# Last columns of the scans kept in SBUF: copied to the states by ScalarE instead of VectorE

## What is computed

```
x = x + ga * attn(layernorm(x) * (1 + ca) + sa)       # attn: Mamba forwards and backwards, then a projection
x = x + gb * ffn(layernorm(x) * (1 + cb) + sb)        # ffn: 6-bit block quantization, then x @ w.T + bias

# one Mamba direction, D_INNER = 1024 channels, N = 16 states for each channel
u     = silu(conv4(h @ win_u.T) + bconv)
dbc   = u @ wx.T                                      # gives dt, B and C
delta = softplus(dt @ wdt.T + bdt)
dA    = exp(delta * A)                                # for each channel and state n
dBu   = delta * u * B                                 # for each channel and state n
h_t   = dA_t * h_(t-1) + dBu_t                        # the scan over the rows t
y     = sum over n of h * C
out   = ((y + u * Dp) * silu(z)) @ wout.T
```

## Time and profile before

| | |
|---|---|
| median of 3 runs | 7603.56 us (7603.14 to 7606.13) |
| the profiled execution | 7600.66 us, its span 7598.7 us |
| busy share: PE / DVE / ACT / POOL | 90% / 92% / 80% / 92% |
| scans, L1153 | 4096; DVE waited 363.1 us for exponentials before them |
| copies from SBUF, L1183 | 1024 |
| dBu, L692 | 2048, 4787.8 us busy on POOL |

### The profile page before, as it was taken

One profiled execution on the slowest core, in us unless ns is written; L12 is line 12 of the kernel. 1 busy time (PEld: TensorE's weight loads), 2 busy tenths in 40 slices (PEclk: granted clock), 3 DMA queues, 4 the chain that ended last, 5 costly groups with the idle time before them and its releaser, 6 DMA issues. The chain is left out here.

```text
span 7598.7 us, 137446 instructions
## 1 busy us (share of the span) xinstructions
PE 6830.6 (90%) x32682; PEld 4035.6 (53%) x32682; DVE 6955.4 (92%) x10093; ACT 6069.6 (80%) x11545; POOL 6968.9 (92%) x3774
## 2 busy tenths in 40 slices
PE   6899999899898989999898999999898999999889
PEld 3455555555555555555555555555555555555455
DVE  2799999999999999999999999999999999999766
ACT  1788888888788888888788888888788888888645
POOL 0899999999999999999999999999999999999678
PEclk8999999999999999999999999999999999999999
DMA  8444445444444454444445544444355444444555
GB/s 258 145 137 134 128 139 149 128 120 144 132 134 126 141 150 124 123 143 138 122 129 145 149 113 136 139 137 134 117 150 149 107 141 135 138 130 131 152 193 172
DMA packets 605609, 1066.02 MB, mean 140 GB/s; under 512 B 113584, under 2 KB 221872, under 8 KB 596336
## 3 DMA queue, kind: packets, MB, share of 16 engines
q1 hardware_dynamic: 602704, 1055.84, 46.9%
q10 hardware_dynamic: 2080, 1.05, 0.0%
HBM read 926.61 MB, written 130.05 MB: 139 GB/s over the span
## 5 line engine op out<-in xcount | busy, mean ns | idle before, releaser
L692 POOL TENSOR_TENSOR dBu<-Bb,du 128x1024 f32<-128x1024 f32 x2048 | 4787.8, 2365 | 74.9 <-DVE hV L1153 44.2
L1153 DVE TENSOR_TENSOR_SCAN scans<-scans,state,dBu 128x512 f32<-128x512 f32 x2304 | 2902.8, 1280 | 393.6 <-ACT scans L806 363.1
L806 ACT ACTIVATE scans<-delta,A 128x512 f32<-128x512 f32 x4096 | 2745.7, 691 | 557.4 <-DVE hC L1169 480.9
L1016 PE MATMUL yT<-ident,hC 128*128 128x128 f32 x9216 | 1407.4, 282 | 344.1 <-DVE hC L1169 340.8
L1169 DVE TENSOR_TENSOR hC<-scans,Cb 128x512 f32<-128x512 f32 x2304 | 1556.8, 680 | 12.2 <-PE yT L1016 12.2
L1016 PEld LDWEIGHTS yT<-ident,hC 128*128 128x128 f32 x9216 | 1058.6, 143 | 774.8 <-DVE hC L1169 536.4
L701 POOL TENSOR_TENSOR hR<-hR,Cb 128x512 f32<-128x512 f32 x1024 | 1290.0, 1270 | 190.2 <-DVE state L1183 183.7
L1153 DVE TENSOR_TENSOR_SCAN hR<-scans,state,dBu 128x512 f32<-128x512 f32 x1024 | 1293.4, 1263 | 0.5
L1009 PE MATMUL bg<-u,comb 128*128 128x512 f32 x2112 | 989.1, 594 | 0.9 <-DVE u L1125 0.9
L1153 DVE TENSOR_TENSOR_SCAN hV<-scans,state,dBu 128x512 f32<-128x512 f32 x768 | 968.6, 1261 | 13.1 <-ACT scans L806 12.8
L948 PE MATMUL bg<-hT,win_u 128*128 128x512 f32 x2112 | 966.5, 598 | 0.9 <-ACT hT L728 0.9
(11 more groups left out here) (163 smaller groups left out, 7586.9 us busy)
## 6 DMA issues: line engine op xcount, KB each, us to landing
comb<-pre_scratch SPq DMA_DIRECT2D x1040, 256.0 KB, 4.6
Bb<-bc_scratch SPq DMA_DIRECT2D x264, 512.0 KB, 8.6
Cb<-bc_scratch SPq DMA_DIRECT2D x264, 512.0 KB, 7.9
win_u<-in_win SPq DMA_DIRECT2D x264, 256.0 KB, 4.9
pre_scratch<-pre SPq DMA_DIRECT2D x264, 256.0 KB, 3.7
comb<-comb_scratch SPq DMA_DIRECT2D x66, 1024.0 KB, 8.0
win_z<-in_win SPq DMA_DIRECT2D x257, 256.0 KB, 2.7
part_scratch<-pre SPq DMA_DIRECT2D x132, 256.0 KB, 2.0
```

The source lines that it names most:

```text
L692: pool.tensor_tensor(dBu[:, q % AHEAD], Bb[:, 2 * q:2 * q + 2, :], du[:, j % 2, :].unsqueeze(1).broadcast_to([P, 2, T]), ALU.mult).then_in ...
L806: act.activation(place(n)[:], delta[:, j % 2, :], ACT.Exp, scale=A[:, v % 2, j * N + n:j * N + n + 1]).then_inc(dA_made, 1)
L1016: ins = nc.tensor.matmul(yT[:, tt * P:(tt + 1) * P], product[:, tt * P:(tt + 1) * P], ident[:], start=first and tt == 0, stop=False, is_tr ...
L1153: nc.vector.tensor_tensor_scan(to, place(n)[:], dBu[:, q % AHEAD, k, :], state[:, c:c + 1], ALU.mult, ALU.add).then_inc(h_made, 1)
```

## The change

The four copies of L1183 go from VectorE's program to ScalarE's. There a copy stands right behind the exponential of the state with a number four higher than the last state it takes: states 3 and 4 behind exponential 8, state 7 behind 11, states 1, 5 and 9 behind 13, state 11 behind 15. It waits for that scan by `h_made`, which the exponential before it has waited for too. The waits on the copies stay as they are: GpSimd's for `aside_saved`, VectorE's and ScalarE's for `turned_saved`.

In SyncE's queue a load of C whose pair has one of the states 3, 4, 7 or 11 no longer waits for GpSimd's product (`hR_made`) but for TensorE having read it (`hR_used`).

```diff
@@ -487,7 +487,7 @@
                         if 2 * q in ASIDE or 2 * q + 1 in ASIDE:
-                            sp.wait_ge(hR_made, aside(last, 2 * q + 2))
+                            sp.wait_ge(hR_used, aside(last, 2 * q + 2) + R0)
                         else:
                             sp.wait_ge(hC_made, straight(last, 2 * q + 2))
@@ -806,6 +806,17 @@
+            def keep_states(g, j, n):
+
+                for ns, places, saved in [(ns, hR, aside_saved) for ns in COPIES] + [(TURNED, hV, turned_saved)]:
+                    if n != ns[-1] + 4:
+                        continue
+                    act.wait_ge(h_made, g * N + ns[-1] + 1 + H0)
+                    k = (ASIDE if places is hR else TURNED).index(ns[0])
+                    step = ns[1] - ns[0] if len(ns) > 1 else 1
+                    act.copy(state[:, j * N + ns[0]:j * N + ns[-1] + 1:step],
+                             places[:, k:k + len(ns), T - 1]).then_inc(saved, 1)
+
@@ -854,6 +865,7 @@
                             step_dA(g, j, v, 2 * q)
+                            keep_states(g, j, 2 * q)
@@ -866,6 +878,7 @@
                             step_dA(g, j, v, 2 * q + 1)
+                            keep_states(g, j, 2 * q + 1)
@@ -1173,15 +1186,6 @@
-                            for n in pair:
-                                for ns, places, saved in [(ns, hR, aside_saved) for ns in COPIES] + [(TURNED, hV, turned_saved)]:
-                                    if n != ns[-1]:
-                                        continue
-                                    dve.wait_ge(h_made, g * N + n + 1 + H0)
-                                    k = (ASIDE if places is hR else TURNED).index(ns[0])
-                                    step = ns[1] - ns[0] if len(ns) > 1 else 1
-                                    nc.vector.tensor_copy(state[:, j * N + ns[0]:j * N + n + 1:step],
-                                                          places[:, k:k + len(ns), T - 1]).then_inc(saved, 1)
```

## The result

The changed kernel is slower: 7649.52 us median (7646.65 to 7664.33), against 7603.35 us for the kernel before on the same chip. The ratio is 1.0066, 95% interval 1.0053 to 1.0078. That is outside the predicted range, 10 us above its upper end. The profiled execution had 7651.53 us with a span of 7649.6 us.

What follows compares the result with a forecast made beforehand. No single bound: VectorE, GpSimd and TensorE run almost evenly. Tiles 4, 3 and 6 gave -0.3 - 0.06 + 0.26 = -0.1 us a chunk, -3 us in all: 7600.5 us, 8-in-10 range 7560 to 7640.

Steps and rivals of the forecast that it cites:

- The offer, 61 + 92 us: VectorE: 1024 undisturbed copies are 61 us, lengthening of copies blocked by GpSimd 92 us; 153 us offered, 2.0% of the span.
- ScalarE's copy, 0.12 us: ScalarE: each copy taken over costs some 0.12 us, at least 0.05 and at most 0.20.
- GpSimd comes late: GpSimd's state 3 product starts 2.5 to 2.7 us late in tiles 7, 0, 4; VectorE's dBu waits some 100 us.
- Rival (a): GpSimd is not the late one, as ScalarE reaches exponential 8 sooner in tiles 7, 0, 4: 60 us, 7543; chance 0.2.
- So tiles 7, 0 and 1 gain nothing ... and lose nothing: Tiles 7, 0, 1: GpSimd's lateness and a VectorE wait take up the 2.2 us offered there; 0 for a chunk.
- the 1.01 us stall of rows 8: Behind tile 1 VectorE waits 1.01 us for tile 2's first exponential anyway; a 0.8 us delay fits in.
- Rival (b): Scan 14's 1.0 us lateness in tile 7 travels on through TensorE: slower by 29 us, 7633; chance 0.25.
- The mark: Sign of lateness through TensorE: scans wait for dBu and scan 0 of tile 2 still waits 1 us for its exponential.
- Tiles 2 and 4: Tile 2: nothing, its closing table load feeds on TensorE; tile 4: net gain 0.3 us, limited by GpSimd's last dBu.
- Tile 6: Scan 10 delayed 0.12 by a ScalarE copy, scan 14 starts 0.2 late behind GpSimd's dBu: net +0.26 us.
- Tile 5: Blocked copy's saving and GpSimd's lateness both end in VectorE's 1.05 us wait ahead of tile 6: 0.
- The load of C, 0: SyncE's load for pair 1 goes out 6.5 us later, covered by GpSimd's wait: 0; if not, 32 us at most.

Runs made afterwards that it cites:

- only_34: Kernel before with only the copy of states 3 and 4 moved to ScalarE, behind exponential 8: 7741.29 us, ratio 1.0166.
- after_filled: Changed kernel plus 36 transposes of zeros on TensorE in tile 7 of every chunk: 7610.89 us, ratio 0.9998 to the kernel before.
- ahead_filled2: Changed kernel, copies before their exponentials, 36 zero transposes in tile 7 and 20 in tile 5: 7572.19 us, ratio 0.9947 to the kernel before.
- load_wait: Kernel before with only the loads of C for pairs 1, 2, 3 and 5 waiting for TensorE's reading of hR: ratio 1.0005.
- bare_dve: Kernel before without the four copies' work, VectorE only raising the semaphores, loads of C as in the changed kernel: 7589.83 us, ratio 0.9965.
- turned_only: Kernel before with only the copy of states 1, 5 and 9 moved to ScalarE: 7594.23 us, ratio 0.9974.
- bare_act: Changed kernel without the copies' work, ScalarE only raising the semaphores at their places: 7582.14 us, ratio 0.9958 to the kernel before.
- ahead: Changed kernel with each copy before the exponential it stood behind: 7596.60 us, ratio 0.9981 to the kernel before.
- all_but_34: Kernel before with copies of 7, 11 and 1-5-9 on ScalarE, 3 and 4 on VectorE, loads of C as changed: ratio 1.0063.

## Why the prediction was wrong

**The offer, 61 + 92 us.** The sizes were read rightly, the second term was not understood. The blocked copies depend on when GpSimd is in an instruction; `only_34` has three times the blocked time of the kernel before with fewer copies on VectorE. And of the 153 us only 27 to 32 arrived when nothing was put in their place.

**ScalarE's copy, 0.12 us.** The record lasts 193 to 202 ns, and its neighbour starts 0.09 us after it (2612.49 and 2612.58). That is within the 0.05 to 0.20, at its lower part. The Trainium skill, "ScalarE: Activation LUTs", section "What ACT_TABLE_LOAD costs", gives an ACTIVATE without pointer operands a fixed 186 ns and 0.833 ns for each element, and an overlap of 93 ns to back-to-back neighbours; the 193 to 202 ns and the two starts agree within some 15 ns.

**GpSimd comes late: right, and sized too small in sum.** The prediction had VectorE waiting for dBu at scan 14, 1.1 us in tile 7, 0.8 in tile 0, the same in tile 1, 0.5 in tile 4, "some 100 us in all". The means are 0.88, 0.55, 0.89 and 0.52 us, and 1.32 more in tile 5, 0.36 in tile 2. Together they are the 145.0 us. Rival (a), that GpSimd would not be late, is out.

**"So tiles 7, 0 and 1 gain nothing ... and lose nothing": the step that failed.** They lose 1.17 us. With the clock restored, in `after_filled`, tile 7 is 0.72 us longer than before, tile 0 is 0.23 shorter and tile 1 0.65 shorter: -0.16 in sum, where the step said 0. So the account of GpSimd and of the 1.01 us stall of rows 8 held for a kernel that keeps its clock; that stall shrinks from a mean of 0.75 to 0.24 us in both kernels, it swallows what it can. The term left out was TensorE's clock. The prediction took TensorE's speed in tile 0 as given. It used PEclk 1.00 of rows 2, which are of tile 1, and gave the clock no term and no rival, though in the kernel before tile 0 of the very rows that it used, 2610.63 to 2636.88 us, has a mean clock of 0.95 and tile 7 ahead of it 0.92. Price: 1.17 + 0.16 = 1.33 us for a chunk, 41 us in all; by the runs, the ratio of 1.0066 against 0.9998 for the filled form.

**Rival (b)** said that the lateness would travel on through TensorE from the point where its reserve in tile 0 is under 0.8 us, at 7633 us. It was the rival nearest to the result, and the time did go through TensorE. But what travelled was not scan 14's lateness: `after_filled` has that lateness nearly unchanged and loses nothing. It was the time that TensorE lost at the lower clock. The mark did not come out either: scan 0 of tile 2 does not still wait 1 us, it waits 0.24; the delay comes out as new waits for exponentials inside tile 1. And its price, 29 us, was under the 46 measured, as it counted only the delay and not the halved clock.

**Tiles 2 and 4** were right: -0.04 for 0 and -0.24 for -0.3, in tile 4 with the forecast 0.5 us wait at scan 14. Tile 3 came out at +0.10 for -0.06. **Tile 6** has the right number, +0.29 for +0.26, by luck: the forecast had scan 14 wait for dBu, and there VectorE hardly waits for it (0.03 us); the time is lost at scan 10, whose wait for its exponential grew from 2.48 to 2.75 us, twice the 0.12 forecast. **Tile 5** was a smaller miss, +0.21 for 0, and +0.36 in `after_filled`: GpSimd's lateness reaches scan 14 there with 1.3 us, and the wait ahead of tile 6 takes in only a part (1.73 to 1.54 us). The low clock in tile 5 (4.07 us of it, 3.53 before) may be a reason, as `ahead_filled2` gains there; in the changed kernel it was not tested.

**The load of C, 0:** right (`load_wait`). **The sum, -0.1 us for a chunk, -3 us in all:** wrong for the kernel that was made. For the one whose TensorE keeps its clock "next to nothing arrives" is right, 0.9998 (0.9988 to 1.0009), but in part by luck: its chunk is some 0.1 us longer than before, and that is the -0.16 of tiles 7, 0 and 1 and the -0.28 of tile 4 against +0.36 in tile 5 and +0.27 in tile 6.

**What stays open.** Why the clock is low in tile 0 in 28 chunks instead of 9. The seven us before tile 0 look alike in their busy time. The kernel before, two chunks that kept the full clock behind them:

```profile
2388.90:2395.90 7.00, 3.64 (x28) 1.00 1.03 414
2819.60:2826.60 7.00, 3.64 (x28) 1.00 1.02 411
```

The changed kernel, three chunks that did not:

```profile
2404.10:2411.10 7.00, 3.91 (x26) 0.96 0.90 328
2620.70:2627.70 7.00, 3.68 (x26) 0.92 0.94 291
3055.10:3062.10 7.00, 3.00 (x18) 0.85 1.02 344
```

In both TensorE is busy for about half of the time; over the span the waits of its matmuls for `hC` and `hR` are no longer in sum than before, since that for `hC` fell to 258.1 us from 340.8 (with the weight loads counted alone it is the same: 515.1 us for both after, 564.6 before):

```profile
PE yT L1029 <- DVE hC L1182: 258.1, 281, 1.9
```

That work in this idle time keeps the clock up is shown by filling it. That the late GpSimd, by the wait for `hR`, is what brings it down is not shown, and `bare_dve` speaks against it as the only way: there TensorE's matmuls do not wait for `hR` at all and its weight loads 6.4 us, and 22 chunks of 31 have a low clock in tile 0. The other kernels without filling lie between: `turned_only` 12, `load_wait` and `bare_act` 14, `ahead` 17, `all_but_34` 20, `only_34` 22. Open too is how much of `bare_act`'s gain is ScalarE's time and how much the earlier release.

## What to carry to other kernels

When a change moves the time at which some engine is done, follow that to TensorE too, and read the granted clock in every stage behind it: where it stands still just ahead of a stretch in which it has nothing to spare, that stretch can run in part at half the clock (tile 0 here: 3.29 us for a chunk instead of 0.76). Before counting a blocked instruction as a saving, ask with what it is in step; moving one instruction out of the rhythm can make its neighbours pay. And move first what no other engine waits for: `turned_only` gained with one copy of four, while every kernel that also moved a copy GpSimd waits for lost (`only_34` 1.0166, `all_but_34` 1.0063, all four 1.0066) until the copies were put one exponential earlier.

## What the runs showed of the hardware that was not expected

- Matmuls that compute nothing made the kernel faster: 1152 of them, 143.5 us of TensorE's time, brought 7649.5 us against 7603.4 (1.0066) down to 0.9998; 640 more in tile 5 went with 0.9964 and then 0.9947, whose intervals overlap. In the kernel before, with little low clock to win back, the same 1152 brought nothing (1.0006).
- A spell at 1.2 GHz that begins in TensorE's idle time reaches on into work that keeps it busy for 5.00 of 5.00 us: the five us then hold 20 to 27 matmuls instead of 31.
- A copy of three columns on VectorE, 0.15 us when undisturbed, had a mean of 1226 ns in one kernel and 350 in another, with the same instruction and only the phase between VectorE and GpSimd changed. The same copy on ScalarE took 202 ns beside the same GpSimd work.
